# Expert-slot loops unrolled into straight code, expert numbers read in fours, output stored by quarters

## The reference

```python
# layer 0: gates over the two best experts, GELU experts of hidden width 256
y = sum_e gates[:, e] * (gelu(z @ W1[e] + b1[e]) @ W2[e] + b2[e]);  x = x + y
# layer 1: shared SwiGLU expert for all tokens, and the two best of 8 SwiGLU experts
out = swiglu(xf, sWg, sWu, sWd)
for e in range(8): out = out + w[:, e:e+1] * swiglu(xf, Wg[e], Wu[e], Wd[e])
```

## Time and profile before

| | |
|---|---|
| median of 3 runs | 667.5 us (664.09 to 671.33) |
| profiled execution | 668.11 us, its span 666.3 us |
| busy share of the span | PE 70%, PE weight loads 57%, DVE 48%, POOL 43%, ACT 33% |
| mean granted TensorE clock | 0.807 |
| layer 0 slots, first to last result scatter issued | 142.8 to 287.3 us |
| layer 1 slots, the same | 486.9 to 629.2 us |

### The profile page before, as it was taken

One profiled execution on the slowest core, in us unless ns is written; L12 is line 12 of the kernel. 1 busy time (PEld: TensorE's weight loads), 2 busy tenths in 40 slices (PEclk: granted clock), 3 DMA queues, 4 the chain that ended last, 5 costly groups with the idle time before them and its releaser, 6 DMA issues.

```text
span 666.3 us, 10763 instructions
## 1 busy us (share of the span) xinstructions
PE 464.3 (70%) x2457; PEld 379.1 (57%) x2458; DVE 322.6 (48%) x1226; ACT 219.5 (33%) x675; POOL 288.3 (43%) x298
## 2 busy tenths in 40 slices
PE   4886563286767768759978889886496976968500
PEld 2564352165656656647867779765375865756400
DVE  5885565245354535511755555357154543535360
ACT  1211140054344435425643444330053442434200
POOL 3075575624344444521354654356144443535500
PEclk9866755788798789879977887668699897989955
DMA  7941112142122221124110110002322221211172
GB/s 181 350 128 36 44 49 68 49 102 68 49 71 65 60 64 40 41 87 150 41 33 24 33 33 21 21 32 69 92 57 73 54 71 45 78 50 44 41 279 95
DMA packets 48132, 49.82 MB, mean 75 GB/s; under 512 B 8331, under 2 KB 37206, under 8 KB 47958
## 3 DMA queue, kind: packets, MB, share of 16 engines
q1 hardware_dynamic: 37942, 29.12, 15.7%
q0 software_dynamic: 8704, 17.97, 8.1%
q10 hardware_dynamic: 1440, 2.18, 0.9%
HBM read 28.00 MB, written 21.25 MB: 74 GB/s over the span
## 4 chain that ended last, share of the span: by engine, by line
PE 57%; issue 12%; DVE 9%; another core or an unknown queue 5%; DMA 5%; POOL 4%; ACT 2%; SPq 2%; ACTq 0%; DVEq 0%; POOLq 0%
PE banks L1061 47%; PE banks L1065 7%; POOL regions L417 3%; DMA parts<-results 3%; PE banks L1129 3%; ACT hT L530 1%; DVE hT L956 1%; DVE parts L691 1%; SPq L320 1%; DMA results<-stream,y_dest 1%; DVE stream L716 1%; SPq L295 1%; ACT hT L613 1%; DMA hT<-regions 1%
## 5 line engine op out<-in xcount | busy, mean ns | idle before, releaser
L436 POOL DMA_INDIRECT results<-stream,y_dest x144 | 138.3, 960 | 181.4 <-DVE stream L863 147.9
L417 POOL DMA_INDIRECT regions<-first_w,pos x64 | 62.3, 973 | 75.2 <-issue 75.2
L417 POOL DMA_INDIRECT regions<-parts,pos x64 | 63.7, 995 | 47.9 <-issue 32.4
L1129 PE MATMUL banks<-const_sb,hT 128*128 128x128 f32 x144 | 44.1, 306 | 47.2 <-issue 31.2
L1061 PE MATMUL banks<-first_w,hT 128*128 x288 | 52.1, 310 | 29.3 <-ACT hT L517 17.7
L1061 PEld LDWEIGHTS banks<-hT,wh 128*128 128x128 f32 x256 | 49.1, 227 | 33.6 <-ACT hT L530 21.2
L1065 PE MATMUL banks<-const_sb,hT 128*128 128x128 f32 x288 | 59.5, 291 | 11.8 <-DVE hT L956 11.3
L1061 PE MATMUL banks<-hT,wh 128*128 128x32 f32 x256 | 54.1, 297 | 17.5 <-ACT hT L530 12.7
L530 ACT ACTIVATE hT<-banks,pcol 128x32 f32<-128x32 f32 x128 | 36.8, 288 | 78.8 <-PE banks L1061 57.2
L1061 PEld LDWEIGHTS banks<-first_w,hT 128*128 128x128 f32 x288 | 43.5, 216 | 33.8 <-issue 33.6
L1065 PEld LDWEIGHTS banks<-const_sb,hT 128*128 128x128 f32 x288 | 42.3, 151 | 35.4 <-DVE hT L956 17.0
(11 more groups left out here) (157 smaller groups left out, 955.2 us busy)
## 6 DMA issues: line engine op xcount, KB each, us to landing
hT<-regions SPq DMA_DIRECT2D x144, 65.0 KB
parts<-results SPq DMA_DIRECT2D x16, 512.0 KB, 4.4
results<-stream,y_dest POOLq DMA_INDIRECT x144
out<-base ACTq DMA_DIRECT2D x8, 256.0 KB
base<-in_x SPq DMA_DIRECT2D x12, 128.0 KB, 3.3
regions<-const_sb SPq DMA_DIRECT2D x18, 65.0 KB
first_w<-in_L_ffn_W SPq DMA_DIRECT2D x1, 1024.0 KB, 7.2
first_w<-in_L_ffn_W SPq DMA_DIRECT2D x2, 512.0 KB, 8.9
```

Source lines behind the costliest of these rows:

```text
L417: pool.indirect_dma_start(regions[layer], bass.IndirectOffsetOnAxis(ap=poss[layer][q][:, t, k:k + 1], axis=0), hrows[layer][:, q, t, k, :] ...
L436: pool.indirect_dma_start(results[layer], bass.IndirectOffsetOnAxis(ap=y_dest[:, out_slot:out_slot + 1], axis=0), y_row[:, out_slot, :], N ...
L1129: nc.tensor.transpose(turned_ps[:, s % 2, 0:P], rows[:, s, 0:D], ident).then_inc(turned[layer], 1)
```

## The change

- The four passes are gone: every engine's program has the 72 slots one after the other, with constants for slot numbers and for the values that waits compare with. SP's loop over the result blocks of layer 0 is straight code too.
- `table_values` reads four values at a time (`Quads`): columns 0, 4, 8, ... of the expert numbers, 72, 76, ... of the first rows, and the eight region ends from column 144 (they began at 147). The three empty columns are gone. PE and DVE ask for the next four at every fourth slot, behind that slot's first product (PE) or its gated result (DVE), two to three slots ahead of use; SP reads four when it comes to the first of them.
- PE's first three row turns of a layer come before its first table read (two before).
- The final stores are four a block, 64 KB from 32 partitions each: SP issues quarters 0 and 1, ACT quarters 2 and 3. SP does it behind all its loads of `parts`.

```diff
+class Quads:
+    def __init__(self, load):
+        self.load, self.values = load, []
+
+    def ready(self, j):
+        while len(self.values) <= min(j, SLOTS - 1):
+            self.values += self.load(len(self.values))
+        return self.values[j]
...
+        def store_rows(eng, n, quarters):
+
+            eng.wait_ge(summed, n + 1)
+            for q in quarters:
+                eng.dma_start(y_rows[n][q], base[q * B:(q + 1) * B, n, :]).then_inc(y_out, 16)
...
             def slot_rows(layer):
                 sp.wait_ge(table_ready[layer], 1)
-                load_rows(layer, 0, False)
-                with sp.Fori(1, SLOTS // UNROLL) as it:
-                    load_rows(layer, it, True)
+                quads = Quads(lambda at: table_values(sp, layer, ROWS_AT_COL + at, QUAD, PAD_ROWS))
+                quads.ready(0)
+                for sent in scattered[layer]:
+                    sp.wait_ge(sent, 16 * TOK // P * TOPK // 2)
+                sp.wait_ge(pads_done[layer], 16 * (E + 1))
+                for j in range(SLOTS):
+                    row = quads.ready(j)
+                    if j >= ROWS_RING:
+                        sp.wait_ge(y_ready[layer], j - ROWS_RING + 1)
+                    sp.dma_start(rows[:, j % ROWS_RING, :], regions[layer][bass.ds(row, P), :]).then_inc(rows_in[j % ROWS_RING], 16)
...
-            sp.wait_ge(y_out, NB * 16)
+            for n in range(NB):
+                store_rows(sp, n, (0, 1))
+            sp.wait_ge(y_out, NB * 4 * 16)
...
             for n in range(NB):
-                act.wait_ge(summed, n + 1)
-                act.dma_start(y_rows[n], base[:, n, :]).then_inc(y_out, 16)
+                store_rows(act, n, (2, 3))
...
+            def slots0():
+                lag = DOWN_LAG[0]
+                experts = Quads(lambda at: table_values(dve, 0, at, QUAD, E - 1))
+                for j in range(SLOTS + lag):
+                    if j < SLOTS:
+                        add_bias(j, experts.ready(j))
+                    if j >= lag:
+                        gate_result(0, j - lag, experts.ready(j - lag))
+                    if j % QUAD == 1 and j + QUAD < SLOTS:
+                        experts.ready(j + QUAD)
...
+            def all_slots(layer):
                 lag = DOWN_LAG[layer]
+                experts = Quads(lambda at: table_values(pe, layer, at, QUAD, E - 1))
+                turn_rows(layer, 0)
+                turn_rows(layer, 1)
+                for j in range(SLOTS + lag):
+                    if j + 2 < SLOTS:
+                        turn_rows(layer, j + 2)
+                    if j < SLOTS:
+                        (gate_and_up if layer else hidden_slot)(j, experts.ready(j))
+                    if j % QUAD == 1 and j + QUAD < SLOTS:
+                        experts.ready(j + QUAD)
+                    if lag - 1 <= j < SLOTS + lag - 1:
+                        turn_act(layer, j - lag + 1)
+                    if j >= lag:
+                        slot_down(layer, j - lag, experts.ready(j - lag))
```

More of the change, by code:

```diff
@@ L127, in __call__ @@
         ins.then_inc(self.sem, 1)
[L128 to L131 removed]
+        self.eng.wait_ge(self.sem, self.n)
 def constant_tables():
@@ L429, in scatter_results @@
             def scatter_results(layer):
[L431 to L437, removed]
+                for j in range(SLOTS):
+                    pool.wait_ge(y_ready[layer], j + 1)
+                    pool.sem_inc(scatter_go, 1)
+                    out_slot = j % OUT_RING
+                    pool.indirect_dma_start(results[layer], bass.IndirectOffsetOnAxis(ap=y_dest[:, out_slot:out_slot + 1], axis=0),
+                                            y_row[:, out_slot, :], None).then_inc(results_out[layer][out_slot], 16)
             pool.wait_ge(scond_ready, 1)
@@ L648, in _ @@
             load_tables(ACT.Gelu)
[L649 to L656, removed]
+            slots0()
             load_tables(ACT.Silu)
@@ L1043, in _ @@
             last_block(NB - 1, (NB - 1) % 2)
-            split_turned(0, 0, True)
-            split_turned(1, 1, True)
-            slots1(0, first=True)
-            with dve.Fori(1, SLOTS // UNROLL - 1) as it:
-                slots1(it)
-            slots1(SLOTS // UNROLL - 1, last=True)
-            for s in range(UNROLL - DOWN_LAG[1], UNROLL):
-                gate_result(1, SLOTS // UNROLL - 1, s)
+            slots1()
             for n in range(NB):
@@ L1128, in turn_rows, with hidden_slot @@
                     pe.wait_ge(state_ready[layer], j - 1)
[L1129 to L1131 removed]
+                nc.tensor.transpose(turned_ps[:, j % 2, 0:P], rows[:, slot, 0:D], ident).then_inc(turned[layer], 1)
+            def hidden_slot(j, e):
                 pe.wait_ge(state_ready[0], j + 1)
[L1133 removed]
+                if j >= 2:
                     pe.wait_ge(biased, j - 1)
[L1135 removed]
@@ L1146, in turn_act @@
-            def turn_act(layer, j, s, first):
+                mm(up_ps[:, j % 2, :], state_hi[:, j % 2, :], wgu_hi[:, expert], stop=False)
+                mm(up_ps[:, j % 2, :], state_hi[:, j % 2, :], wgu_lo[:, expert], start=False, stop=False)
+                mm(up_ps[:, j % 2, :], state_lo[:, j % 2, :], wgu_hi[:, expert], start=False).then_inc(up_ready[1], 1)
+            def turn_act(layer, j):
                 pe.wait_ge(slot_act[layer], j + 1)
-                if not (first and s < 2):
+                if j >= 2:
@@ L1149, in turn_act, with slot_down @@
                     pe.wait_ge(act_copied[layer], j - 1)
-                turn(act_turned_ps[:, s % 2, :], [act_row[:, s % 2, c * P:(c + 1) * P] for c in range(NC)], act_turned[layer])
-            def slot_down(layer, j, s, e, first):
+                turn(act_turned_ps[:, j % 2, :], [act_row[:, j % 2, c * P:(c + 1) * P] for c in range(NC)], act_turned[layer])
+            def slot_down(layer, j, e):
                 pe.wait_ge(act_copied[layer], j + 1)
-                if not (first and s < 2):
+                if j >= 2:
```

211 lines of the change are left out of this document (78 added, 133 removed).

## The result

| | before | changed |
|---|---|---|
| median, in turn on one chip | 665.8 us (660.8 to 671.3, 4 runs) | 613.4 us (609.1 to 619.1, 4 runs) |
| profiled execution, its span | 668.11 us, 666.3 us | 619.05 us, 617.3 us |
| first to last result scatter, layer 0 | 144.5 us | 129.7 us |
| last of layer 0 to first of layer 1 | 199.5 us | 198.4 us |
| first to last, layer 1 | 142.3 us | 122.8 us |

The ratio is 0.9215, 95% interval 0.910 to 0.933. Forecast were 621 us and a range of 604 to 641. The profiled execution is the longest of its four runs, so its stages are read here against the profiled execution of before, as in the prediction's sum. Of 49.0 us between the spans, 14.8 lie in layer 0's slots, 19.5 in layer 1's, 15.2 behind the last scatter and 1.1 between the layers; the first scatter of layer 0 comes 1.7 us later.

What follows compares the result with a forecast made beforehand. PE's long table reads at pass boundaries, followed by a half clock, and a store-only tail were taken to cost time; no engine is full within passes. Savings 26.2 + 6.7 + 14.0 = 46.9 us from 668.1 give 621.2, said as 621, range 604 to 641.

Steps and rivals of the forecast that it cites:

- The slot loops: Both layers' slot stages: boundary steps removed for 32.3 us less, reads of four give 6.1 back, net 26.2 us less.
- bare reads: Slot stages: a quarter of 54 reads of four, at 0.45 us each, left uncovered, 6.1 us back.
- The pace: Slot stages: straight passes' pace kept, 1.785 us a slot in layer 0 and 1.80 in layer 1, 126.7 and 127.8 us.
- The entries: Start of each layer's slots: shorter first reads and a third early row turn on PE, 6.7 us less in sum.
- The end: Final stores: all 16 DMA engines share them, tail 3.8 us in place of 15.8, end 14.0 us earlier (10 to 16).
- Dear reads: Slot stages: a read of four costs 0.98 us, half of it bare, 26.5 us instead of 6.1, so 641; chance 0.12.
- Stores without gain: Final stores: something other than the number of engines sets 102 GB/s, so 635 us; chance 0.08.
- The larger gain (604): Slots and end: reads wholly hidden, slots at the last passes' 1.76 and 1.70 us, stores at 16, 604 us; chance 0.12.
- The half clock throughout: Both slot stages: frequent reads idle PE and keep its clock at 1.2 GHz, 80 us more, 701; chance 0.03.
- three signs: Slots: no PE "issue" stretch over 1 us, no mid-stage window at clock 0.5, 127 and 128 us between first and last scatter.

Runs made afterwards that it cites:

- e7: Changed kernel with one empty table column first, so reads of four begin at columns one above a multiple of four: 608.57 us, ratio 0.9074.
- e4: Changed kernel, straight code, but each engine reads 18 table values in one instruction when it comes to the first of them: 536.36 us, ratio 0.9486.
- e6: Changed kernel, straight code and new stores, but with the table and long reads of before, read when first needed: 644.16 us, ratio 0.9682.
- e5: Changed kernel unaltered, run again on a chip where the kernel before takes 664 us: 612.47 us, ratio 0.9234.
- e1: Kernel before with only the final stores changed, four a block, two quarters each from SP and ACT: 552.86 us, ratio 0.9749.
- e2: Against e1, ACT alone issues all four quarters of a block and SP issues no store: 553.82 us, ratio 0.9786.
- e9: Changed kernel unaltered, on a chip where the kernel before takes 564 us: 509.09 us, ratio 0.9017.
- e8: Changed kernel with slot results stored by plain DMAs from SP instead of POOL's scatters to the tokens' rows: 542.34 us, ratio 0.816.
- e12: The kernel of e8 again, on a chip where the kernel before takes 566 us: 500.42 us, ratio 0.8847.

## Why the prediction was right, and where its terms were off

**The slot loops.** The step was right, and a little too careful. Forecast: 126.7 and 127.8 us and 6.1 for bare reads, 260.6 in all; measured 129.7 + 122.8 = 252.5, a gain of 34.3 us and not 26.2. Of the 8.1 us missed, 6.1 are the price of the reads: 0.33 us, not 0.45, and nothing of it bare as far as e7 tells, where even reads of 1.0 us cost nothing on such a chip. The other 2 are the pace. The reading of the earlier trace rows, that columns divisible by four are read in fours, is confirmed by e4 and e7. e6 adds what the prediction left undivided: of the 35 to 37 us that loops and reads brought on that chip (e5's 51.5 less 15 to 17 for the stores), the short early reads have about 32.

**The pace.** Layer 0 came 3 us slower and layer 1 5 us faster than its pace, and the prediction named this as its weakest point. Its choice to keep the straight passes' pace, with its unexplained waits, instead of PE's 1.21 us a slot gave the right time on this chip. That is in part luck: the cause of the waits was unknown, nothing said that straight code would keep them, and the misses of the two layers (3 and 5 us) have opposite signs. On a chip of 565 us the pace is 89.8/71 = 1.27 us in layer 0 (POOL's 0.96 + 0.30) and 1.46 in layer 1 (PE), and the gain is 9.8% instead of 7.8%. The pace that it took from its rows does not carry over from one chip to another.

**The entries.** 6.7 us were forecast. Layer 0: 0.8 us less from PE's first read to the first scatter (8.45 to 7.63) for 1.4, and the stage ahead began its slots later. Layer 1: 5.3 forecast, 1.1 seen in the first profile. The mechanism was right; the chain of e5 has no read left, and the entry from SP's read on is 4.7 us shorter even in the first profile. The rest was given back ahead of it, where the chain shows the table waiting for ACT, and ACT for PE's product. Over that stretch e5 gains 10.5 us, and on the chips of 565 us the changed kernel (163.1) gains 6.4 on e1 (169.5).

**The end.** 14.0 forecast, 15.2 between last scatter and end. The tail took 3.5 us for 3.8. e2 confirms the reason: the new stores give the bandwidth with one issuer too, the second issuer gives about 2 us of the tail and no difference in the median that is clear of noise. The last add, forecast at 19.3 us behind the last scatter, ended 18.4 behind it.

**The rivals.** Dear reads: the price comes true in e7, the cost does not. Stores without gain: false by e1. The larger gain (604) is what the fastest run of e5 reached. The half clock throughout: layer 1's slots ran at 1.00 and layer 0's mean stayed at 0.93, with no table read of PE or DVE over 0.6 us left in it. Of what was to show the forecast right, three signs failed. The chain still has "issue" of up to 2.1 us inside the slots. Layer 0 has five stretches at 0.50 in mid-stage, where e9 has none before its last 4 us and e7, on a chip with the waits, has one (from 159.0 us); what brings them beyond the waits is open. And the slots took 129.7 and 122.8 us for 127 and 128.

**The sum.** 621.2 us were forecast for the profiled execution, which took 619.05. That it came so near is luck in part, since two misses cancel in it: the slots came 8.1 us better, the entries 7.3 worse, and the end 1.2 better.

## What to carry to other kernels

Read run-time values into registers in small groups that start at a column divisible by four, a few slots ahead. Reads of 5 us blocked PE's issue here and were followed by a granted clock of 0.50, while the loop around them cost 0.7% at most. When a DMA's tail runs at a quarter of the bandwidth, look at its outermost dimension before adding issuers (e1 and e2). When a consumer idles with its producer long done, look at what a third engine is doing in that moment, and run the same kernel on a second chip before trusting the pace.

## What was not expected of the hardware

On some chips the engines that wait for PE's products start late while POOL sends indirect DMAs one behind the other. The kernel before took 564 to 566 us in three of the batches, and 664 to 666 in the other one and in the runs of the result; the changed kernel took 509 and 612 to 613. Slot stages with POOL's scatters cost 125.5 + 123.7 us on the one kind and 89.8 + 103.8 on the other; without them 84.8 + 103.2 on both. That the scatters are the cause is shown by e8 and e12, though not whether it is POOL's issuing or the indirect transfers themselves. That it is the news of PE's results that is held is read from timelines like the one above and was not tested by itself. It does not simply last until the scatters pause: of the 16 times that DVE's L861 started over 0.5 us late in layer 1's slots in the first profile of after, 4 lie within 0.05 us of the end of a scatter and the other 12 between 0.6 and 1.4 us behind one. What distinguishes the chips, and whether scatters that are spaced out avoid it, stays open.

On PE a read of four values into registers took 0.33 us from a column divisible by four and 1.00 from columns one above that (e7); one of 18 took 1.6 to 1.8 us from columns divisible by four and 4.5 to 4.6 from columns two above that (e4).
